# A four-layer convolution and attention kernel: block-diagonal products as two 64x64 tiles of the array

## The reference, cut to what matters

```python
x = swin_block(x)      # layernorm, 7x7 shifted-window attention with 3 heads, layernorm, 24->96->24 GELU MLP
x = conv_block(x)      # layernorm, 24->48, 3x3 convolution 48->24, silu
t = tokens(x)
for l in (2, 3):
    t = t + fft_mixer_l(_ln_t(t))   # 24->48, relu, FFT over 3136 tokens, complex scale, relu, inverse FFT, 48->24
    t = t + ffn_l(_ln_t(t))         # 24->96->24 with values rounded to 8-bit floats
```

## Time and profile before

| | |
|---|---|
| median of 3 runs | 3613.85 us (3609.70 to 3615.42) |
| profiled execution | 3627.03 us, of it 3625.2 us from the first to the last instruction |
| mean granted TensorE clock | 0.965 of full speed |
| PE busy | 3165.1 us (87%), 46700 records |
| DVE, ACT busy | 1811.8 us (50%), 1647.0 us (45%) |
| chain that ended last | PE 73%, ACT 11%, DVE 6%, issue 4%, SP's queue 3%, DMA 2% |

### The profile page before, as it was taken

How to read it: one execution, slowest core, us unless ns; L and a number is a source line. 1 busy time by engine, 2 the same in 40 slices (tenths; PEclk the granted TensorE clock), 3 DMA queues, 4 the chain that set the end, 5 groups by cost and what they waited for, 6 DMA issues and landing times.

```text
span 3625.2 us, 105949 instructions
## 1 busy us (share of the span) xinstructions
PE 3165.1 (87%) x46700; PEld 2100.8 (58%) x46700; DVE 1811.8 (50%) x2898; ACT 1647.0 (45%) x3027; POOL 217.3 (6%) x462
## 2 busy tenths in 40 slices
PE   6978889888898898988989889898889988898888
PEld 4536646467465575555755647546466474664755
DVE  5525555354643546445563445634456255563455
ACT  3543354533555425554345443453444535445344
POOL 4510000000000000000000000000000000000000
PEclk8999999999999999999999999999999999999999
DMA  2321000110001100110001100011000110001100
GB/s 77 66 55 41 2 15 7 46 31 2 15 19 37 26 2 16 32 38 12 2 16 34 46 1 2 17 49 31 1 2 17 49 31 1 1 17 31 31 1 15
DMA packets 31236, 84.55 MB, mean 23 GB/s; under 512 B 24818, under 2 KB 25954, under 8 KB 26930
## 3 DMA queue, kind: packets, MB, share of 16 engines
q1 hardware_dynamic: 29506, 72.56, 8.4%
q0 software_dynamic: 1280, 5.21, 0.5%
HBM read 61.70 MB, written 14.84 MB: 21 GB/s over the span
## 4 chain that ended last, share of the span: by engine, by line
PE 73%; ACT 11%; DVE 6%; issue 4%; SPq 3%; DMA 2%; ACTq 0%; DVEq 0%
PE ps L1096 73%; ACT lv L692 3%; ACT rs L697 3%; SPq L487 2%; DVE area_ty L917 2%; DMA area_hz<-f_all 1%; DVE xs L1065 1%; DMA area_ty<-area_hz 1%; SPq L502 1%; ACT area_ty L778 1%; ACT area_ty L784 1%; ACT sq L684 1%; DVE area_ty L1061 0%; DVE area_ty L1037 0%; ACT area_ty L826 0%
## 5 line engine op out<-in xcount | busy, mean ns | idle before, releaser
L917 DVE TENSOR_TENSOR area_ty<-ps,rs 128x448 f32<-128x448 f32 (+2 forms) x416 | 285.3, 686 | 479.5 <-ACT rs L697 479.4
L1096 PE MATMUL ps<-area_hz 32*64 32x147 f32 (+2 forms) x7180 | 368.7, 292 | 88.2 <-DVE area_hz L955 35.1
L1096 PE MATMUL ps<-area_ty,area_hz 113*64 113x49 f32 (+1 forms) x10240 | 394.4, 250 | 19.5 <-DMA area_ty<-area_hz 16.7
L1096 PE MATMUL ps<-sq,keep_sb 128*128 128x448 f32 (+1 forms) x832 | 380.0, 557 | 31.8 <-ACT sq L684 25.4
L1096 PEld LDWEIGHTS ps<-area_hz 32*64 32x64 f32 (+2 forms) x7180 | 296.4, 158 | 186.9 <-issue 164.1
L802 ACT ACTIVATE area_hz<-ps 121x384 f32<-121x384 f32 (+2 forms) x256 | 129.8, 520 | 580.6 <-PE ps L1096 580.6
L1096 PEld LDWEIGHTS ps<-area_ty,area_hz 113*64 113x64 f32 (+1 forms) x10240 | 333.1, 135 | 98.9 <-issue 98.7
L692 ACT ACTIVATE lv<-ps 128x448 f32<-128x448 f32 (+1 forms) x416 | 218.1, 524 | 334.2 <-PE ps L1096 331.2
L938 DVE TENSOR_REDUCE area_hz<-ps 113x12 f32<-113x588 f32 x256 | 197.0, 770 | 285.1 <-PE ps L1096 284.5
L1096 PE MATMUL ps<-area_ty,g_sb 56*112 56x192 f32 (+1 forms) x3712 | 311.4, 321 | 25.9 <-DVE area_ty L1037 19.7
L1096 PE MATMUL ps<-xs,keep_sb 128*128 128x448 f32 x560 | 266.3, 569 | 67.4 <-DVE xs L1065 36.5
(11 more groups left out here) (114 smaller groups left out, 4084.6 us busy)
## 6 DMA issues: line engine op xcount, KB each, us to landing
area_hz<-f_all SPq DMA_DIRECT2D x16, 2541.0 KB
xw<-x_in SPq DMA_DIRECT2D x8, 1568.0 KB, 7.2
y_out<-xs SPq DMA_DIRECT2D x32, 252.0 KB
f_all<-piece POOLq DMA_DIRECT2D x16, 317.6 KB, 3.3
area_ty<-area_hz SPq DMA_DIRECT2D x256, 4.6 KB
area_hz<-raw_in SPq DMA_DIRECT2D x1, 2894.0 KB, 9.5
g_sb<-g_in SPq DMA_DIRECT2D x6, 355.2 KB
g_sb<-g_in SPq DMA_DIRECT2D x2, 710.5 KB
```

The source lines that it names most:

```text
L917: ve.tensor_tensor(o, a, b, ALU.mult, **kw).then_inc(normed, 1)
L1096: return pe.matmul(o, a, b, start=start, stop=stop)
```

## The change: what it does

Each of the six products above becomes two: rows 0 to 63 of the weights' upper left 64x64 quarter with rows 0 to 63 of the moving operand, into partitions 0 to 63 of the bank; and the lower right quarter with rows 64 to 127, into partitions 64 to 127. The two quarters that are left out hold only zeros. The semaphore is raised by the second. The waits stand where they stood. `keep_busy`, the fp8 products, the mixer and everything on other engines stay.

```diff
+BLOCK = 64
...
+            def blocks(bank, w, still, moving):
+
+                for o in range(0, 128, BLOCK):
+                    r = slice(o, o + BLOCK)
+                    ins = mm(ps[r, bank, 0:w], still[r, r], moving[r, :])
+                return ins
...
-                mm(ps[:, center_bank(k), 0:w], K("center"), src[:, w * i:w * i + w]
-                   ).then_inc(centered, 1)
+                blocks(center_bank(k), w, K("center"), src[:, w * i:w * i + w]).then_inc(centered, 1)
...
-                mm(ps[:, variance_bank(k), 0:w], K("variance"), sq[:, k % 2, 0:w]
-                   ).then_inc(var_made, 1)
+                blocks(variance_bank(k), w, K("variance"), sq[:, k % 2, 0:w]).then_inc(var_made, 1)
...
-                mm(ps[:, key_bank(0), 0:TW], wk[:, :], xt).then_inc(k_made, 1)
-                mm(ps[:, query_bank(0), 0:TW], wq[:, :], xt).then_inc(q_made, 1)
+                blocks(key_bank(0), TW, wk, xt).then_inc(k_made, 1)
+                blocks(query_bank(0), TW, wq, xt).then_inc(q_made, 1)
...
-                        mm(ps[:, 7, 0:TW], wk[:, :], xt).then_inc(k_made, 1)
+                        blocks(7, TW, wk, xt).then_inc(k_made, 1)
...
-                        mm(ps[:, 6, 0:TW], wq[:, :], xt).then_inc(q_made, 1)
+                        blocks(6, TW, wq, xt).then_inc(q_made, 1)
...
-                        mm(ps[:, 5, 0:TW], spread[:, :], osb[:, (t - 1) % 2, :]).then_inc(sum_spread, 1)
+                        blocks(5, TW, spread, osb[:, (t - 1) % 2, :]).then_inc(sum_spread, 1)
...
-                        mm(ps[:, 5, 0:TW], K("wo"), osn[:, (t - 1) % 2, :]).then_inc(projected, 1)
+                        blocks(5, TW, K("wo"), osn[:, (t - 1) % 2, :]).then_inc(projected, 1)
```

## The result

| | before | after |
|---|---|---|
| median, 4 runs each | 3614.24 us (3609.70 to 3615.42) | 3586.73 us (3582.79 to 3589.80) |
| profiled execution, span | 3627.03, 3625.2 us | 3582.79, 3581.0 us |
| granted clock, mean of that execution | 0.965 | 0.975 |

The changed kernel takes 0.9926 of the time [0.9908 to 0.9943], 27.5 us less. Predicted were 3603 us and 11 us less: the direction was right, the size was not.

What follows compares the result with a forecast made beforehand. PE was taken to bound the kernel, though not everywhere alike, most clearly in window attention. -16.1 - 3.8 + 8.4 + 0.5 = -11.0 us, from the median 3613.85 to 3603 us; range 3594 to 3610, with rivals 3592 to 3626.

Steps and rivals of the forecast that it cites:

- The sum of own work: All stages: smaller exposed weight loads save 16.1 and 3.8 us, new changes of shape cost 8.4 and 0.5; -11.0 us.
- Attention -10.1: Window attention, all quads: 9.6 us saved at entries from another shape without a wait, 0.5 at waits.
- convolution and first mixer about -4: Norms there: 6 entries a quad saving 0.048 us and 11 after a wait saving 0.02, x 8.
- ffns +3.4: Both ffns: gain 4.2 and 1.3 us from smaller loads but pay 8.9 for new changes of shape.
- 1.2 were predicted: Window attention at 1.00 clock: 25 entries x 0.048 us, the stage 1.2 us shorter of 125.60.
- the predicted 0.048: Each entry from another shape without a wait: load 0.058 us shorter, second half's load 0.01 more, 0.048 saved.
- the change from fp8 to center: Ffn slots: a new change of shape costing 0.15 us, on the path in 7 slots a quad, +8.4 us.
- the predicted 0.1: Ffn 1: each slot was to become 0.1 us longer.
- the predicted 0.07 shorter: Ffn 0: each later slot was to become 0.07 us shorter.
- queueing: Every split product: second half starts only behind the first's first record, 0.37 us later; +290, 3900 us; chance 0.02.
- another bound: Window attention: PE's savings given back waiting for DVE's maxima or ACT; -9.6 falls away, 3612 us; chance 0.14.
- the first rival: Ffn slots and norm chains around the MLP: lower clock, slower with 16 to 24 stretches, +8 to +18; chance 0.28, 0.12 slower.

Runs made afterwards that it cites:

- e1_attention_only: Kernel before with halves only in window attention, its projections and the norm before the MLP; 3604.6 us, ratio 0.9958.
- g2_conv_mix0: Kernel before with halves only in the norms of the convolution and the first mixer; 3614.3 us, ratio 1.0003.
- e2_ffn_only: Kernel before with halves only in the norms computed inside the ffns' slots; 3608.1 us, ratio 0.9985.
- e6_columns: Changed kernel with two products of all 128 rows x 64 columns in place of the two 64x64; 3563.0 us, ratio 0.9846.
- e4_quarters: Changed kernel with four 32x32 tiles on the diagonal in place of two 64x64; 3588.6 us, ratio 0.9929.
- g1: Kernel before with halves only in the center products of the ffns' own norms; 3621.7 us, ratio 1.0024.
- g3: Changed kernel with two 128x64 products in window attention, 64x64 left elsewhere; 3555.6 us, ratio 0.9843.
- f1: Changed kernel with 128x32 strips in the ffns' own norms, 32x32 tiles in convolution and first mixer norms, 128x64 elsewhere; 3559.8 us, ratio 0.9856.
- h3: Kernel before with halves only in window attention, its norm and the centers of the ffns' own norms; 3613.6 us, ratio 0.9991.
- e3: Kernel before with halves only in the second norm's variance products in the ffns' slots, off the path; 3620.9 us, ratio 1.0013.
- e5: Changed kernel with whole products again in the norms computed inside the ffns' slots; 3609.6 us, ratio 0.9972.
- e7: Kernel before with one 128x128 `keep_busy` product added behind each mixer's opening wait; 3628.8 us, ratio 1.0033.
- e8: Changed kernel with whole centers but halved variances in the ffns' slots; 3599.9 us, ratio 0.9948.
- h2: Changed kernel with the ffns' own centers as two whole-array products, half the tokens each, one behind the other; 3610.3 us, ratio 0.9976.
- h4: Changed kernel with the ffns' own centers whole, one 64x64 product of 8 tokens ahead of each; 3638.2 us, ratio 1.0058.

## Why the prediction was wrong in size, step by step

**The sum of own work held, within its uncertainty.** -11.0 predicted, -12.2 at one clock. Attention -10.1 against -14.0 (e1_attention_only); convolution and first mixer about -4 against -3.3 (g2_conv_mix0); ffns +3.4 against +1.5 (e2_ffn_only). That the totals come within 1.2 us is partly luck, as the parts measured alone add up to -15.8. Stages at one clock speak for the sum without any price: the quads whose attention had 0.99 took 123.08 us there on average before (three of eight) and 121.78 after (four of eight), 1.3 less where 1.2 were predicted, with 0.4 either way for the rounding of that clock; ffn 0 became 0.29 shorter, ffn 1 0.55 longer. From start to start the `wk` and `wq` step fell by 0.05 us (1437.85 to 1440.81 in the trace of before, 1419.81 to 1422.72 after), the predicted 0.048; the change from fp8 to center cost 0.15 by the start of the down products, as predicted (1351.07 to 1353.29 is 2.22, 1368.38 to 1370.45 was 2.07), of it 0.10 ahead of the center and the rest in the halves themselves; ffn 1's slot, from one group of up products to the next, went from 6.14 (1368.38 to 1374.52) to 6.25 (1351.07 to 1357.32), the predicted 0.1; the ffn 0 slot that starts at 1226.45 is 6.94 us long, where the one from 1249.11 to 1256.14 took 7.03, the predicted 0.07 shorter within 0.02. The halves do run side by side: the first records of the center at 1351.73 start 0.007 us apart, where under 0.04 was forecast. And PE does bound attention: the rivals of queueing and of another bound fell.

**The step that failed is the clock.** The forecast set "the mean clock still near 0.965", a change of 0, and the only case it priced for the clock was the first rival, which "ends slower" because "the halves fill half" of the array. Measured: 0.9745, 50 us less at the lower level, x 0.35 = -17.4 us, by this estimate the larger part of the gain. The premise was wrong. e6_columns fills all rows and columns and e4_quarters a quarter of the array, and both have the halves' clock (0.9743, 0.9732). The price per us that the rival used, 0.2 to 0.45, was right.

**Where the clock came from.** From the centers in the ffns' slots. With the ffns' own centers split side by side (after, e2, e4, e6, g1, g3, f1, h3), the mean clock was 0.971 to 0.975 and 0 of 56 starts of ffn 1 were at the lower level; with these whole, marked or in pieces (before, e1, e3, e5, e7, e8, g2, h2, h4), 0.966 to 0.968 and 24 of 63. With the last quad's ffn 1, which the table leaves out, it is 0 of 64 and 26 of 72. They are enough for part of it (g1, -7.6) and no kernel without them has more than -1.7 of it (e1, e5, e8, h2: -1.7 to +1.2). That one center behind the other is not enough (h2) and that a change of shape is not it (h4) was shown; why side by side makes the difference was not.

**Whether the starts of ffn 1 only fell otherwise in time.** This rival can be answered from the traces. In each of them the granted level changes only at evenly spaced times (55 to 101 changes a trace, none more than 0.003 us off). With whole, marked or pieced centers, such a time came 0.51 to 1.00 us after the start of the 5 us stretch at 26 of the 72 starts, and the level fell at all 26; at the other 46 it did not fall. With centers side by side it came there in 23 of 64, and the level never fell. So the difference is in the centers, and not in where the starts happened to lie. The same explains e3_off_path and e7_shift: at none of their 16 starts did such a time come there (the earliest was 1.11 us in), which is the luck of one execution.

**A warning that was in the rows.** That "how much of the array a product fills may matter" rested on one pair of stretches, busy for the same share (2.00 of 3.40, 4.04 of 6.90) and unlike in more than form. One pair gives no sign; the case in which the halves raise the clock belonged beside it, with the same price.

**What stays open.** The parts don't add up in the clock: attention alone has -1.7, the ffns -8.6, the rest +2.2, together -8 where the change has -17.4. It may be that attention's halves help only once the centers are split, but h3's 0.9722 against g1's 0.9708 is too small a step to show it; it does suggest that more than those two is needed for 0.9745. The starts of ffn 1 are also only part of the change's gain: in the two profiled executions about as much lies in ffn 0 (11 of the 13.4 us that it became shorter), and no run isolates that. Nor is it known why e3_off_path fell to 0.9659.

The Trainium skill, "TensorEngine Tiling (Array Packing)", Key Properties, has a change of tiling mode drain the engine, and the prediction weighed that rule against this change. The trace agrees that each change costs, 0.10 us at 1351.73, and e6_columns turns the rule to use: where neighbours share rows and columns it is not paid, -23 us of own work against the halves.

## What to carry to other kernels

Give a small block-diagonal product the shape of the products beside it in the queue, not the smallest tiles that hold its blocks: 128x64 next to 113x64 was worth three times the own work of 64x64 (-35.5 against -12.2 us), all of it in attention; the same idea brought nothing in the ffns, where only part of the neighbours was changed (f1_neighbours_shape). When a change alters how products lie on the array, price the clock with both signs, read the granted clock by place and not only its mean, and compare kernels at one clock before reading small differences. Then own work and clock can be told apart to a few us with a dozen runs.

## What the runs showed of the hardware that was not expected

- The same kernel's mean granted clock varies from run to run, 0.962 to 0.974 over 103 runs, and the time with it, 3598 to 3632 us. It is not noise in the timing: each us more at the lower level goes with 0.35 us more on average, 0.30 to 0.59 in single kernels.
- Two, or four, tiles side by side in the ffns' centers keep a granted clock that one whole product loses after the same quiet stretch (PE busy 0.69, 0.50 and 0.46 us of the three us before): the level fell in 26 of 26 starts of ffn 1 with whole centers and in 0 of 23 with split ones, counted over the starts where one of the trace's times of change came 0.51 to 1.00 us in.
- Entering 128x64 from 113x64 costs 0.11 us less than entering 64x64: 1.34 against 1.45 us from the merged scores' and values' products to `wk`.
